# Who issues the transfers that take a unit's values and sums apart: SyncE in place of ScalarE

## The reference

```
for Wq, bq, Wk, bk, Wv, bv, Wo, bo, gamma, beta in (layer 0, layer 1):
    q = (x @ Wq + bq)   -> 8 groups x 4 heads x 112 x 16
    k = (ctx @ Wk + bk) -> 8 groups x 375 x 16
    v = (ctx @ Wv + bv) -> 8 groups x 375 x 16
    p = softmax(q @ k.T / 4 + mask)
    o = (p @ v) @ Wo + bo + x
    x = (o - mean(o)) * rsqrt(var(o) + 1e-6) * gamma + beta
```

## Time and profile before

| | |
|---|---|
| time, median of 3 runs | 1748.22 us (1747.8 to 1748.25) |
| the profiled execution's own time | 1745.91 us |
| its span in the profile | 1744.0 us |
| TensorE (PE) busy | 1695.7 us, 97% |
| VectorE (DVE) busy | 1254.3 us, 72% |
| ScalarE (ACT) busy | 1041.6 us, 60% |
| GpSimd (POOL) busy | 582.5 us, 33% |
| transfers on SyncE's queue (q1) | 205.82 MB |
| transfers on ScalarE's queue (q10) | 29.38 MB |

### The profile page before, as it was taken

The page is one execution under the profiler, slowest core; times in us unless marked ns, Lnnn a source line. Parts: engine busy times, 40 slices in busy tenths (PEclk is TensorE's granted clock), DMA queues, the critical chain, the costliest instruction groups (busy, mean ns, idle before and its releaser), DMA issues. The chain is left out here.

```text
span 1744.0 us, 35810 instructions
## 1 busy us (share of the span) xinstructions
PE 1695.7 (97%) x10881; PEld 1003.8 (58%) x10881; DVE 1254.3 (72%) x1714; ACT 1041.6 (60%) x2370; POOL 582.5 (33%) x1165
## 2 busy tenths in 40 slices
PE   5899999999999999999999999999999999999996
PEld 3466556566556565556565565565566565565652
DVE  6477777677777677777677776677776777776784
ACT  1465566566566566666566665666665666665663
POOL 2133333333333333333333332333332333332422
PEclk8899999999999999999999999999999999999998
DMA  8556555546545545546555535445544455445431
GB/s 280 149 136 167 145 124 140 137 125 154 147 118 144 136 126 150 149 116 155 140 131 148 142 105 134 127 126 137 138 109 134 121 133 137 137 109 135 116 106 43
DMA packets 287961, 235.87 MB, mean 135 GB/s; under 512 B 140810, under 2 KB 262916, under 8 KB 287140
## 3 DMA queue, kind: packets, MB, share of 16 engines
q1 hardware_dynamic: 267428, 205.82, 44.3%
q10 hardware_dynamic: 20480, 29.38, 6.7%
HBM read 101.39 MB, written 22.02 MB: 71 GB/s over the span
## 5 line engine op out<-in xcount | busy, mean ns | idle before, releaser
L743 DVE TENSOR_REDUCE mx<-ms 128x2 f32<-128x750 f32 x896 | 809.4, 924 | 424.6 <-PE ms L875 418.0
L616 ACT ACTIVATE probs<-sc 125x448 f32<-125x448 f32 x1536 | 750.6, 541 | 288.0 <-PE sc L846 283.7
L875 PE MATMUL ms<-ks,qs 96*128 96x375 bf16 (+1 forms) x2560 | 439.1, 325 | 14.6 <-DVE mx L743 7.7
L846 PE MATMUL sc<-qs,ks 99*125 99x448 bf16 x1536 | 430.7, 357 | 4.6 <-DMA qs<-mT 2.9
L894 PE MATMUL pv<-probs,vs 125*32 125x448 f32 x3072 | 316.6, 545 | 0.0
L846 PEld LDWEIGHTS sc<-qs,ks 99*125 99x125 bf16 x1536 | 191.6, 136 | 204.6 <-ACT probs L616 123.9
L875 PEld LDWEIGHTS ms<-ks,qs 96*128 96x128 bf16 (+1 forms) x2560 | 173.2, 98 | 199.6 <-issue 70.6
L936 PE MATMUL job<-wo,on 128*112 128x512 f32 x512 | 264.2, 598 | 5.7 <-POOL on L525 5.7
L951 PE MATMUL job<-xT,wq 128*128 128x224 f32 x1024 | 218.0, 356 | 0.9 <-ACT qf L656 0.9
L757 DVE RECIPROCAL orec<-osum 128x112 f32<-128x112 f32 x256 | 213.3, 835 | 0.9 <-DMA osum<-oraw 0.9
L951 PEld LDWEIGHTS job<-xT,wq 128*128 128x128 f32 x1024 | 190.6, 190 | 20.9 <-ACT qf L656 8.5
(11 more groups left out here) (53 smaller groups left out, 979.4 us busy)
## 6 DMA issues: line engine op xcount, KB each, us to landing
ctxT<-in_ctxT SPq DMA_DIRECT2D x64, 750.0 KB, 4.9
qs<-qp SPq DMA_DIRECT2D x768, 56.0 KB, 2.5
ks<-kp SPq DMA_DIRECT2D x768, 46.9 KB, 2.8
osum<-oraw ACTq DMA_DIRECT2D x128, 112.0 KB, 2.9
oc<-oraw ACTq DMA_DIRECT2D x128, 112.0 KB, 3.7
mask<-in_mask SPq DMA_DIRECT2D x64, 164.1 KB, 5.7
xT<-in_xT SPq DMA_DIRECT2D x32, 224.0 KB, 4.8
xin<-in_x SPq DMA_DIRECT2D x32, 224.0 KB, 2.9
```

Of the source, the lines that this page charges most:

```text
L616: nc.scalar.activation(probs[0:KCS, k, j, :], sc[j][0:KCS, 0:GL], ACT.Exp)\
L743: nc.vector.tensor_reduce(mx[o][:, cols], ms[n % 2][:, :, 0:S2], AX_X, ALU.max).then_inc(max_done[o], 1)
L846: last = nc.tensor.matmul(sc[j][0:KCS, 0:GL], ks[p][0:KM, g, rows], qs[p][0:KM, g, :], start=True, stop=not masked)
L875: last = nc.tensor.matmul(to, qs[o][0:KT, group, cols], ks[o][0:KT, group, :], start=True, stop=not masked)
```

## The change

ScalarE's `outputs` and its two calls go, with the table `OUT_AT`. SyncE gets the same function. The pair of half 1 stands behind the six transfers of `ks[o]` half 1 and ahead of those of `qs[o]` half 1, and waits for the copy of L624 (`pv_evac`). The pair of half 0 stands behind the last of `qs[p]` half 0 and ahead of the context's load, and waits for `on_ready` and `pv_evac`.

```diff
-OUT_AT = [(11, 1), (9, 1)]
@@ block.sync
+            def outputs(u, h, value):
+                sp.wait_ge(pv_evac[u][h], value)
+                sp.dma_start(osum[64 * h:64 * h + 64, :], oraw[h][1::2, :]).then_inc(sum_in[u], 16)
+                sp.dma_start(oc[64 * h:64 * h + 64, :], oraw[h][0::2, :]).then_inc(o_in[u], 16)
+
@@ slot
                 if a_ok:
                     load_mask(o, ahead, lay[1])
                     stack_terms(o, 1, ks[o], kp[o], 1)
+                if p_ok:
+                    outputs(o, 1, count(post + 1))
+                if a_ok:
                     stack_terms(o, 1, qs[o], qp, 0)
@@
                     stack_terms(p, 0, qs[p], qp, 0, of=(2,))
+                if m_ok:
+                    taken_out, weighted = count(main + 1), count(2 * post + 2)
+                    if p_ok:
+                        sp.wait_ge(on_ready[o], weighted)
+                    outputs(p, 0, taken_out)
                 if more and not (isinstance(ahead, int) and ahead + 1 == 0):
                     load_ctx(o, ahead + 1, lay[3] if not isinstance(ahead, int) else 0 if ahead + 1 < PER else 1)
@@ block.scalar
-                def outputs(u, h, n):
-                    act.wait_ge(pv_evac[u][h], n + 1)
-                    act.dma_start(osum[64 * h:64 * h + 64, :], oraw[h][1::2, :]).then_inc(sum_in[u], 16)
-                    act.dma_start(oc[64 * h:64 * h + 64, :], oraw[h][0::2, :]).then_inc(o_in[u], 16)
-
-                    if k == OUT_AT[p][1] and p_ok:
-                        outputs(o, 1, post)
-                    if k == OUT_AT[p][0] and m_ok:
-                        if p_ok:
-                            act.wait_ge(on_ready[o], 2 * post + 2)
-                        outputs(p, 0, main)
```

## The result

The changed kernel takes 1755.95 us (median of 4 runs, 1752.86 to 1757.67) against 1748.01 us before (4 runs): ratio 1.0041, interval 1.0029 to 1.0053. That is 7.9 us slower. It lies in the range given, 1747 to 1761, but 5 us over the predicted 1751.0, and in the class to which I gave 0.45, not in the one that I took as likeliest. The profiled execution took 1754.6 us with a span of 1752.7, 8.7 longer than before.

A forecast was written before the change was run, and what follows sets the result against it. TensorE, busy 97% of the span, was taken as the bound. Terms 1.2 + 1.0 + 1.0 - 0.1 gave +3.1 us at most; +2.8 was taken, from 1748.22 to 1751.0 us, range 1747.0 to 1761.0.

The forecast's parts named there:

- The bound on the gain: TensorE's mid-kernel waits: 6.5 us at most to win, the change touching only 1.1; ScalarE's freed 2.2 us a slot gain 0.
- The price on SyncE: Four issues and three waits per slot on SyncE: 1.15 and 1.3 us, 2.45 a slot, bounds 1.7 and 2.8.
- rival A: Issues cost on SyncE what they cost on ScalarE: 2.8 us a slot, +7.8 us, 1756.0; chance 0.33.
- No block at the new waits: SyncE's new waits for the copy: 1.1 us to spare at the first place, copy several us old at the second.
- Steps 1 to 4: Slot (1, 12), layer 0: mask 1.3 us later, max_rows 2.45, keys' stacks 1.25, then a 0.1 us stall.
- Step 4: Last query stack, layer 0 loop: lands in 2.35 us instead of 3.5, stall 0.1 us, 1.2 us over 12 slots.
- Step 5: Unrolled layer 0 slots with turned stores: last query stack costs 1.0 us in (1, 14), 1.0 in the other three together.
- rival C: Context lands last, up to 0.86 us later: 0.7 us stall in 30 slots, +21 us, 1769; chance 0.07.
- Step 2: Half 1 of slot (1, 12): max_rows lands at 722.25, needed at 722.44; 0.2 us remain, no stall.
- Step 6: Layer 1, without turned stores: 2 us more waiting in the slot, keys' stacks don't move, 0 us.
- Step 7: p = 0 slots cost 0 us; in the last slots SyncE issues about 0.1 us sooner than ScalarE, -0.1 us.
- The signs: Pair 0.47 and 0.50, mask 1.3 us later, landing 2.4, waits for qs up 2 to 4 us, none for ctxT.

The follow-up runs named there:

- e8: Kernel before, with ScalarE issuing half 0's pair in piece 10 instead of 9 in p = 1 slots; ratio 1.0002 to the kernel before.
- e3: Both pairs issued by SyncE in the looped slots only, by ScalarE in the unrolled ones; ratio 1.0025 to the kernel before.
- e4: Both pairs issued by SyncE in the unrolled slots only, by ScalarE in the loops; ratio 1.0039 to the kernel before.
- e9: The changed kernel run and profiled again, nothing else changed; 1755.54 us, ratio 1.0046 to the kernel before.

## Why the prediction was right or wrong

**The bound on the gain** (6.5 us, no gain from ScalarE) held. ScalarE got 2.2 us a slot back and TensorE's waits for it did not change.

**The price on SyncE.** 0.59 + 0.60 at the first place, 0.53 + 0.60 at the second, with steps 1.28 and 1.32 us: 2.6 a slot, where I took 2.45 and gave 1.7 to 2.8. The first place was 0.13 over. The two issues alone, 1.13 to 1.19 us, are over my 0.97 and over rival A's 1.09; A's 0.62 for the second was the better row than SyncE's own 0.50 for a plain store. The slot's 2.6 lies between my 2.45 and A's 2.8, and over the 2.5 from which A was to decide.

**No block at the new waits** held in the repeating slots.

**Steps 1 to 4** held in kind and nearly in size. Mask 1.32 later (1.3), `max_rows` 2.60 (2.45), keys' stacks 1.37 (1.25), landing 2.4 instead of 3.5 (2.35), stall 0.16 (0.1). Step 4's shortening of the landing is shown by e8, whose only change is ScalarE's time of issue. Without it, step 4 would have been 1.1 us more a period. The rule of the Trainium skill ("DMA: Bandwidth & Descriptors", Queues, rings and completion order) that I leaned on there agrees with that run. For the loop I had 1.2 us and it was 3.0: 1.8 in the 11 repeating periods, where each stall was 0.06 longer than I took it, and 1.2 in the first. I had taken all twelve as alike. The first is not: the kernel before already waits 0.4 us for a stack there. It is not the unrolled slots' new issues that make it late either, for in e3, which has none of those, the same period loses 1.9 us, and in e4, which has only those, nothing. Why SyncE has less room in it is open.

**Step 5 failed.** I put 2.0 us on the unrolled slots, for the last query stack alone, and 1.0 of it on (1, 14). They cost 5.8, by the markers 3.6 at three contexts, 1.2 at stacks and 1.0 at `max_rows`. In (1, 14) the stack cost nothing: the marker moves by less than 0.01 us over that boundary. The 1.35 us were lost 20 us earlier, on the context:

```profile
828.59 1.50 PE L925 MATMUL pv<-ctxT,wk 128*128 128x375 f32 x4 [1.11 <-DMA ctxT<-in_ctxT]
```

It was issued 1.3 us later, as expected, but took 7.0 us to land, not the 5.3 of the earlier trace rows which I carried from the loop to every slot; before it took 6.0 at this place. That delay of TensorE then gave SyncE the time it needed for the stack, which landed at 846.7 and was needed at 847.2; without the delay that would have been 845.9. In (1, 0) too the context was late and the stack was not. So rival C's mechanism was real, in three slots (five in e9) rather than in the 30 that I priced it for, while in the loops the load landed in 4.1 to 5.6 us and TensorE has no wait for it in this profile. I had checked the loop for all three needs and the unrolled slots for one.

**Step 2's 0.2 us** for `max_rows` was enough in the loops but for slot (1, 18), in the first period of the second one, and not in (1, 0), (1, 15) and (1, 17): 1.2 us in 4 waits. **Step 6** held but for this wait of 0.3 us and 0.2 at one slot further on.

**Step 7, the end.** -0.1 was predicted. The profiles show 1.0 us lost in slot (1, 30), where `max_rows` was late, and 1.8 gained from the last marker (10.5 us late) to the end of the span; most of the gain is not the change's: the last output projection runs 6.54 us before and 5.11 after, at another clock (below).

**The additions.** Mid-run, half 1's pair cost 0.5, half 0's 2.2, both 9.0 us. In the slot read, one pair fits into what SyncE waits and two do not. That the lateness would pile up from slot to slot is not what the trace shows: the mask loads of (1, 12), (1, 14) and (1, 16) are 1.3 us late against TensorE, as step 1 has it.

**The signs.** Of what I had said would show it, the mask's 1.3 us, the landing of 2.4 us and the growth of the waits for `qs` (2.5 us) came; the row of the pair at 0.47 and 0.50 did not, nor the 1 us of stack behind (1, 14), and there were waits for `ctxT`. So the time lies in the range although the loop's term was less than half of what was lost there and the unrolled slots' about a third; the range was wide enough because A had stretched it, and that the misses stayed inside is in part luck. Rival A's 1756.0 is the measured time to 0.1 us by luck: it had 4.8 us in the loop, where 3.0 were lost, 3.4 in the unrolled slots, where 5.8 were, and nothing for the context.

What stays open: which share of the 3.3 us in the first unrolled slots belongs to the weight loads that SyncE issues there as well, what makes the context take 6 to 7 us in (1, 14), and why the slots in which it is late differ from one profile of the kernel after to the next.

## What to carry to other kernels

When issues are moved to a queue, add up that queue's waits slot by slot, and take the slots that differ (unrolled ones, changes of phase) separately, with every transfer that someone waits for behind the new place: with 1.3 us of room one pair of issues of 1.3 us was free, the other alone cost 4.5 us, and both cost 8 us.

The issue's time on the sequencer was the same for 32 KB and 112 KB of one pattern (0.60 us). Take it from the same transfer on another engine (0.47 and 0.62 us here, for 0.55 and 0.60) rather than from another transfer on the same one (0.35 and 0.50).

Look at what else is in flight before moving a transfer in time: a landing of 3.5 us was 2.3 once a pair from another engine was issued 1.3 us later.

## What the runs showed of the hardware

TensorE's clock in the last output projection differed between the two profiled executions. Windows of before, ahead of the last 5.7 us wait for GpSimd and behind it (the column behind the busy times is the granted clock):

```profile
1722.80:1725.30 2.50, 2.42 (x25) 0.64 (x24) 2.32 (x6) 0.01 (x1) 0.52 (x1) 1.00 0.00 0
1730.90:1737.50 6.60, 6.54 (x8) 2.31 (x8) 0.53 (x1) 0.00 (x0) 0.66 (x1) 0.55 0.02 5
```

and of after:

```profile
1733.00:1735.40 2.40, 2.39 (x24) 0.60 (x24) 2.25 (x6) 0.00 (x0) 0.46 (x1) 1.00 0.00 0
1741.00:1746.30 5.30, 5.11 (x8) 1.92 (x8) 0.63 (x2) 0.00 (x0) 0.66 (x1) 0.72 0.01 3
```

Both ran at the upper level (2.4 GHz) until the wait and partly at the lower one (1.2 GHz) behind it, for most of the projection before and for about half of it after. The eight matmuls and all ahead of them are the same; it moved the span by 1.4 us.

The start varies more than I had allowed for: the marker of 62.45 us started between that and 66.05 us in the thirteen profiles (before, after and the eleven runs), and the kernel before itself ran from 1743.3 to 1750.7 us beside the experiments. One profile's span does not tell 2 us.
